# Token sums of squares by ones products over channel-major squares, with root and reciprocal on the spread values, in a two-layer transformer kernel on one core

## The chip, the cores and the metric

The kernel runs on 1 core of a Trainium2 chip. The metric is the device time of one execution in microseconds (us). The profiler names the engines PE (TensorE matmuls; PEld is its weight load), DVE (VectorE), ACT (ScalarE), POOL (GpSimd) and SP (the queue that issues the DMAs).

## The reference, cut to what matters

Two layers work on 1024 tokens of 256 channels. The second layer's MLP block contains an attention of its own, and that attention reads the layer-normalised activations after a second, root-mean-square normalisation:

```
h = _layernorm(x, axis=-1) * (1 + cb) + sb
x = x + gb * _L1_ffn_ref(h, ...)

def _L1_ffn_ref(hidden_states, ln1_w, ln2_w, Wq, ...):
    def _rmsnorm(x, w):
        v = jnp.mean(x * x, axis=-1, keepdims=True)
        return x * jax.lax.rsqrt(v + EPS) * w        # EPS = 1e-6
    x = _rmsnorm(hidden_states, ln1_w)
    attn = _attention(x, Wq, Wk, Wv, Wo)             # 16 heads, causal
    ...
    h = _rmsnorm(residual, ln2_w)
```

So one number per token is needed, 1 / sqrt(mean of its 256 squares + 1e-6), and it multiplies all channels of that token, before the q, k and v projections of this attention and again before the MLP.

## The kernel before, in words

Each engine has one program, written out in order, and the engines meet at semaphores (`S["name"]`, counted up by `then_inc`, awaited by `wait_ge`). There is no scheduler: the order in the code is the order on each engine. Only inside an attention is the order made by a small planner (`ORDER`), which the change leaves alone.

Activations live in two layouts. Token-major: 128 partitions are tokens, the channels lie along the row (`x`, `xn`). Channel-major: 128 partitions are channels, two chunks `dt` of 128 channels, 1024 tokens along the row, worked on in two halves of 512 tokens (`hT`, `h_hi`, `h_lo`, `rb`). The fp32 projections are made of three products of a high part and a low part (`mm3`, with `h_hi`, `h_lo`, `w_hi`, `w_lo`).

The place in question is `layer_norm(3)` and what follows it, ahead of `attention(1)`. DVE normalises `xn` (L1106), PE transposes it (L459), and ACT adds scale and shift and leaves channel-major `hT` in four pieces of 128 x 512 (L885; semaphore `ln_f`). Then the root-mean-square is taken:

1. PE transposes `hT` back to token-major (L819, 16 transposes, `u_t`).
2. ACT squares each of the 8 token tiles from PSUM, with an accumulated sum into a column of `ss` (L1050, `ss_ok`).
3. DVE makes mean + 1e-6 (L1457), ACT takes the root (L1053), DVE the reciprocal (L1459), all on 128 x 8 values.
4. DVE multiplies the identity by each tile's column (L1462, 8 times, `dg`), which gives diagonal matrices in `t1`; PE multiplies a matrix of ones by them (L824, `rb_m`), which spreads the value of each token over all 128 partitions; ACT copies that to `rb` (L1056, `rb_ok`).

Then `scaled_product` on DVE (L1210) makes `t2` = `hT` x `ln1_w` x `rb`, ACT rounds it to `h_hi` (L1060), and `scaled_low` on DVE (L1218) makes `h_lo`. For the first half PE waits until both its chunks have an `h_lo`:

```
for w in range(8):
    half, dt, is_k = w // 4, (w // 2) % 2, w % 2
    pe.wait_ge(S["ln_hl"], 12 + 2 * half + 2)
```

The eight products `w` (three kinds of row in each, L437 to L439) are q and k. Each is split into three bf16 parts (ACT L931 and L921, DVE L1193 and L1200), and SP writes the parts to a scratch in DRAM (L382) and loads them back in the layout of the attention (L391, 12 DMAs for a pair). PE meanwhile makes v (`token_major`) and then starts `attention(1)`, whose first matmuls (L743, L766) wait for those DMAs.

Of the kernel before, what the change touches and what calls it, by code (L numbers as in the profile page):

```python
# [7 lines left out]
ALU = mybir.AluOpType  # L8
ACT = mybir.ActivationFunctionType
# [7 lines left out]
P = 128  # L17
T = 1024
D = 256
H = 16  # L20
DH = D // H
NT = T // P
KC = D // P
HALF = 512
# [163 lines left out]
def build(nc, a, out):  # L188
# [13 lines left out]
    with ctx:  # L202
        def sb(name, shape, dt=F32):
            return ctx.enter_context(nc.sbuf_tensor(name, shape, dt))
# [4 lines left out]
        def overlay(*groups):  # L209
# [15 lines left out]
        hT = sb("hT", [P, KC, T])  # L225
# [31 lines left out]
        t1 = sb("t1", [P, 2, HALF])  # L257
        t2 = sb("t2", [P, 2, HALF])
# [18 lines left out]
        ve = sb("ve", [P, NT])  # L277
        sd = sb("sd", [P, NT])
        rs = sb("rs", [P, NT])
        ss = sb("ss", [P, NT])  # L280
        ident = sb("ident", [P, P])
        identb = sb("identb", [P, P], BF16)
        ones = sb("ones", [P, P])
        bd = sb("bd", [P, VW])
        minus1 = sb("minus1", [P, 1])
        tri = sb("tri", [P, P], BF16)
        rc = sb("rc", [P, 2, 2, 8])
        mx = sb("mx", [P, 2, 4, 4, 2])
# [13 lines left out]
        bank = [psum[:, i, :] for i in range(8)]  # L302
# [10 lines left out]
            att_t at_e wo_m ysem bt x_upd  # L313
            qt sp_h sp_r sp_m sp_l pw0 pw1 qr_ld0 qr_ld1 qr_ld2 qr_ld3 vp_e
            p1_s p1_mx m_max m_step m_t m_c m_ld0 m_ld1 s2 ex pv ob ot at_r
            u_t ss_ok ss_ve ss_sd ss_rs dg rb_m rb_ok a_f a_hi_s woa_m woa_ok ab
            z_m z_ok ha_m mm_f mm_h mm_ok bst h_f h_hi_s h_ok fs
            dq w_sc wf_t wf_h wf_l g_m u_m gl_s it_s it_h it_l fdn out_done""".split()
        names += [f"nat{i}" for i in range(FC[1])]
        S = {n: sem(n) for n in names}  # L320
# [112 lines left out]
        def _(pe):  # L433
# [148 lines left out]
            for j in range(4):  # L582
                m = modulation(wmod0, 0, 5, j)
# [11 lines left out]
            for t in range(NT):  # L595
# [8 lines left out]
                m = modulation(wmod0, 0, 3, 4 + t)  # L604
# [45 lines left out]
            for c in range(16):  # L650
                if c % 2 == 0 and c >= 4:
# [3 lines left out]
                    m = modulation(wmod1, 1, 7, (c - 4) // 2)  # L655
# [24 lines left out]
            for j in range(6, 12):  # L680
                m = modulation(wmod1, 1, 3, j)
# [20 lines left out]
            for w in range(8):  # L702
                half, dt, is_k = w // 4, (w // 2) % 2, w % 2
# [3 lines left out]
                for j in range(4):  # L707
                    c0 = is_k * D + dt * P
                    m = pe.transpose(bank[w % 4][:, j * P:(j + 1) * P], qk[:, 4 * half + j, c0:c0 + P], ident[:, :])
# [95 lines left out]
            for kc in range(KC):  # L805
                for o in range(KC):
                    m = pe.matmul(bank[1][:, kc * 96:(kc + 1) * 96], raw[:, 3, o, kc * P:(kc + 1) * P],
                                  a_rep[:, o, :], start=o == 0, stop=o == KC - 1)
# [3 lines left out]
            layer_norm(3)  # L812
            pe.wait_ge(S["wt_lo"], 10)
            pe.wait_ge(S["woa_ok"], 1)
            for v in range(4):
                pe.wait_ge(S["ln_f"], 12 + 2 * (v // 2) + 2)
                for j in range(2):
                    for dt in range(KC):
                        m = pe.transpose(bank[4 + v][:, j * D + dt * P:j * D + (dt + 1) * P],  # L819
                                         hT[:, dt, (2 * v + j) * P:(2 * v + j + 1) * P], ident[:, :])  # L820
                m.then_inc(S["u_t"], 1)
            for half in range(2):
                pe.wait_ge(S["dg"], 4 * half + 4)
                pe.matmul(bank[4 + half][:, :], ones[:, :], t1[:, half, :], start=True, stop=True  # L824
                          ).then_inc(S["rb_m"], 1)
            for w in range(8):
                half, dt, is_k = w // 4, (w // 2) % 2, w % 2
                pe.wait_ge(S["ln_hl"], 12 + 2 * half + 2)
# [2 lines left out]
                tok = slice(half * HALF, (half + 1) * HALF)  # L831
# [2 lines left out]
                    m = mm3(bank[w % 4][:, :], w_hi[:, kc, c0:c0 + P], w_lo[:, kc, c0:c0 + P],  # L834
                            h_hi[:, kc, tok], h_lo[:, kc, tok], kc == 0, kc == KC - 1)
                m.then_inc(S["qt"], 1)
            pe.wait_ge(S["rb_ok"], 2)
            for t in range(NT):
                if t >= 2:
                    pe.wait_ge(S["vp_e"], 8 + t - 1)  # L840
# [7 lines left out]
            for half in range(2):  # L848
                pe.wait_ge(S["h_ok"], 2 * half + 2)
                tok = slice(half * HALF, (half + 1) * HALF)  # L850
# [17 lines left out]
        def _(act):  # L868
# [174 lines left out]
            act.copy(woa[:, :, :], bank[1][:, 0:192].rearrange("p (c k) -> p c k", c=KC)).then_inc(S["woa_ok"], 1)  # L1043
            layer_norm_std(3)
            layer_norm_mod(3)
            for t in range(NT):
                act.wait_ge(S["u_t"], t // 2 + 1)
                if t >= 2:
                    act.wait_ge(S["ss_ok"], t - 1)
                act.activation(t2[:, t % 2, 0:D], bank[4 + t // 2][:, (t % 2) * D:(t % 2 + 1) * D], ACT.Square,  # L1050
                               accum_out=ss[:, t:t + 1]).then_inc(S["ss_ok"], 1)
            act.wait_ge(S["ss_ve"], 1)
            act.activation(sd[:, :], ve[:, :], ACT.Sqrt).then_inc(S["ss_sd"], 1)  # L1053
            for half in range(2):
                act.wait_ge(S["rb_m"], half + 1)
                act.copy(rb[:, half * HALF:(half + 1) * HALF], bank[4 + half][:, :]).then_inc(S["rb_ok"], 1)  # L1056
            for u in range(4):
                half, dt = divmod(u, 2)
                act.wait_ge(S["a_f"], u + 1)
# [18 lines left out]
        def _(ve_):  # L1078
            dve = ve_
# [373 lines left out]
            weight_lo(11, 9, 2 * D)  # L1453
            layer_norm(3)

            dve.wait_ge(S["ss_ok"], 8)
            dve.tensor_scalar(ve[:, :], ss[:, :], 1.0 / D, 1e-6, ALU.mult, ALU.add).then_inc(S["ss_ve"], 1)  # L1457
            dve.wait_ge(S["ss_sd"], 1)
            dve.reciprocal(rs[:, :], sd[:, :]).then_inc(S["ss_rs"], 1)  # L1459
            dve.wait_ge(S["ss_rs"], 1)  # L1460
            for t in range(NT):
                dve.tensor_scalar(t1[:, t // 4, (t % 4) * P:(t % 4 + 1) * P], ident[:, :], rs[:, t:t + 1], None, ALU.mult  # L1462
                                  ).then_inc(S["dg"], 1)

            for u in range(5):
                if u < 4:
# [28 lines left out]
        def _(pool):  # L1495
            pool.memset(ident[:, :], 0.0).then_inc(S["idz"], 1)
            pool.memset(bd[:, :], 1.0).then_inc(S["idz"], 1)
            pool.memset(minus1[:, :], -1.0)
            pool.memset(tri[:, :], 0.0).then_inc(S["idz"], 1)
            pool.wait_ge(S["idz"], 3)  # L1500
            pool.affine_select(out=ident[:, :], in_=ident[:, :], compare_op=ALU.not_equal, fill=1.0, base=0,
# [154 lines left out]
```

## Time and profile before

| | |
|---|---|
| median of 3 runs | 780.99 us (780.71 to 781.37) |
| the profiled execution: its own time | 780.97 us |
| its span, from first to last instruction | 779.4 us |
| PE busy | 676.7 us, 87% |
| DVE busy | 481.4 us, 62% |
| ACT busy | 334.0 us, 43% |
| POOL busy | 168.3 us, 22% |
| mean granted TensorE clock | 0.912 |

The span leaves 1.6 us of the execution's own time outside it. The granted clock is a share of 2.4 GHz, so 0.50 is 1.2 GHz. The shares of busy time are averages over stages that have different limits; the stage changed here lasts from about 509 to 529 us. An fp32 matmul of 128 x 512 stands as two records in the trace.

### The profile page before, as it was taken

Reading aid. Unit: us, or ns where it says so; the run is one execution under the profiler, and the core shown is the slowest. Engines: PE = TensorE matmul, PEld = TensorE weight load, DVE = VectorE, ACT = ScalarE, POOL = GpSimd, SP = SyncE. Lnnn points to the kernel's source line nnn. Section 1 sums busy time; section 2 is a strip of 40 time slices with the busy share of each in tenths; the row PEclk is TensorE's granted clock in tenths of the full one; section 3 lists DMA queues with packets and bytes.
Section 4 is the critical chain, followed back from the end, with each engine's and each line's share of the span. In section 5 each row is a group of like instructions: output and inputs, shape, how many; then the busy total and the mean of one; then the engine's idle time right before and its main releaser. Section 6 shows DMA issues by size and latency. Waiting matters only on the chain.

```text
span 779.4 us, 10833 instructions
## 1 busy us (share of the span) xinstructions
PE 676.7 (87%) x4017; PEld 447.2 (57%) x4017; DVE 481.4 (62%) x975; ACT 334.0 (43%) x539; POOL 168.3 (22%) x222
## 2 busy tenths in 40 slices
PE   5857996899999986747999998768799999999996
PEld 4645774677777775623544443447355444368885
DVE  5794367566666627966898850546688888232223
ACT  4213023433333342332555667456155566943332
POOL 1251122344455532910000000000000001002221
PEclk9995568999999997958999999969799999999999
DMA  9930001000000000066200000005730000050001
GB/s 215 245 114 1 0 2 54 1 1 0 1 1 1 0 1 1 6 191 210 84 2 1 1 2 1 0 1 162 229 98 2 1 1 1 3 162 1 1 1 54
DMA packets 47040, 36.18 MB, mean 46 GB/s; under 512 B 16206, under 2 KB 44892, under 8 KB 46988
## 3 DMA queue, kind: packets, MB, share of 16 engines
q1 hardware_dynamic: 46988, 35.49, 15.6%
q8 instruction: 32, 0.52, 0.3%
q14 instruction: 20, 0.16, 0.1%
HBM read 27.94 MB, written 7.34 MB: 45 GB/s over the span
## 4 chain that ended last, share of the span: by engine, by line
PE 42%; issue 21%; POOL 12%; DVE 11%; SPq 7%; DMA 3%; ACT 3%; POOLq 0%; DVEq 0%; ACTq 0%
PE psum L780 8%; POOL it_lo L1576 8%; PE psum L743 7%; PE psum L766 7%; SPq L391 4%; POOL wd L1559 3%; PE psum L627 2%; DVE qk L1172 2%; PE psum L639 2%; SPq L328 2%; PE psum L437 2%; PE psum L483 2%; PE psum L769 2%; DMA parts_scratch<-parts 2%; PE psum L439 2%
## 5 line engine op out<-in xcount | busy, mean ns | idle before, releaser
L957 ACT ACTIVATE pt<-psum 128x1024 f32<-128x1024 f32 (+1 forms) x192 | 147.9, 811 | 101.1 <-PE psum L769 72.6
L1256 DVE TENSOR_REDUCE mx<-psum 128x1 f32<-128x512 f32 (+3 forms) x216 | 132.6, 665 | 17.4 <-PE psum L743 8.9
L743 PE MATMUL psum<-kr,qr 96*128 96x512 bf16 (+3 forms) x384 | 111.1, 339 | 15.9 <-DMA kr<-parts_scratch 12.4
L766 PE MATMUL psum<-qr,kr 99*128 99x512 bf16 (+3 forms) x384 | 100.0, 333 | 9.2 <-DMA qr<-m3T 7.8
L1576 POOL TENSOR_TENSOR it_lo<-it,it_hi 128x512 fp32r<-128x512 f32 x48 | 67.1, 1398 | 165.5 <-ACT it_hi L995 164.3
L743 PEld LDWEIGHTS psum<-kr,qr 96*128 96x128 bf16 x384 | 37.0, 100 | 79.2 <-DVE mx L1256 30.5
L780 PE MATMUL psum<-pt,vp 128*32 128x512 f32 (+3 forms) x768 | 81.7, 498 | 0.0
L437 PE MATMUL psum<-h_hi,wf_hi 128*128 128x512 f32 x192 | 78.3, 408 | 3.1 <-issue 3.1
L439 PE MATMUL psum<-h_hi,wf_lo 128*128 128x512 f32 x192 | 75.5, 393 | 0.0
L438 PE MATMUL psum<-h_lo,wf_hi 128*128 128x512 f32 x192 | 75.3, 392 | 0.0
L1602 POOL TENSOR_SCALAR m<-m 128x16 bf16<-128x16 f32 x16 | 4.1, 254 | 307.0 <-DVE m L1256 153.5
L1326 DVE TENSOR_TENSOR it<-psum,gl 128x512 f32<-128x512 f32 x48 | 33.2, 691 | 60.0 <-PE psum L439 47.3
L1256 DVE TENSOR_REDUCE m<-psum 128x1 f32<-128x384 f32 (+3 forms) x88 | 50.9, 636 | 29.7 <-PE psum L746 29.1
L766 PEld LDWEIGHTS psum<-qr,kr 99*128 99x128 bf16 x384 | 35.9, 99 | 49.9 <-ACT pt L957 22.4
L995 ACT CAST it_hi<-it 128x512 fp32r<-128x512 f32 x48 | 29.8, 620 | 75.1 <-DVE it L1326 75.1
L1315 DVE TENSOR_TENSOR wf_lo<-psum,wf_hi 128x512 fp32r<-128x512 f32 (+1 forms) x48 | 24.5, 553 | 48.6 <-ACT wf_hi L981 48.6
L746 PE MATMUL psum<-tri,identb 128*128 128x128 bf16 x256 | 52.2, 230 | 0.0
L769 PE MATMUL psum<-identb,tri 128*128 128x128 bf16 x256 | 51.2, 223 | 0.0
L991 ACT ACTIVATE gl<-psum 128x512 f32<-128x512 f32 x48 | 28.7, 598 | 52.0 <-PE psum L439 33.9
L1533 POOL TENSOR_TENSOR t<-qk,rope_s 128x256 f32<-128x256 f32 x32 | 34.5, 1098 | 57.1 <-DVE qk L1353 23.5
L437 PEld LDWEIGHTS psum<-h_hi,wf_hi 128*128 128x128 f32 x192 | 36.5, 190 | 10.5 <-issue 3.6
L439 PEld LDWEIGHTS psum<-h_hi,wf_lo 128*128 128x128 f32 x192 | 36.4, 189 | 8.1
(194 smaller groups left out, 1203.9 us busy)
## 6 DMA issues: line engine op xcount, KB each, us to landing
parts_scratch<-parts SPq DMA_DIRECT2D x16, 384.0 KB, 3.3
qr<-parts_scratch SPq DMA_DIRECT2D x48, 128.0 KB, 2.6
kr<-parts_scratch SPq DMA_DIRECT2D x48, 128.0 KB, 2.6
wmod<-in_L_wmod SPq DMA_DIRECT2D x1, 1536.0 KB, 6.1
x<-in_L_attn_x SPq DMA_DIRECT2D x2, 512.0 KB, 4.0
wmod<-in_L_wmod SPq DMA_DIRECT2D x1, 1024.0 KB, 6.2
packed<-in_L_ffn_down_W_packed SPq DMA_DIRECT2D x1, 1024.0 KB, 10.1
nat<-in_L_ffn_W_in_base SPq DMA_DIRECT2D x8, 128.0 KB, 2.6
```

Of the source, the lines that this page charges most:

```text
L437: pe.matmul(dst, st_hi, mv_hi, start=first, stop=False)
L438: pe.matmul(dst, st_hi, mv_lo, start=False, stop=False)
L439: return pe.matmul(dst, st_lo, mv_hi, start=False, stop=last)
L743: m = pe.matmul(b, qr[0:PARTS_ROWS, c, h, (qt - 4 * c) * P:(qt - 4 * c + 1) * P], kr[0:PARTS_ROWS, ch, h, 0:w], start=True, stop=not diag)
L746: m = pe.matmul(b[:, w - P:w], identb[:, :], tri[:, :], start=False, stop=True)
L766: m = pe.matmul(bank[4 + 2 * at[0] + j][:, 0:w], kr[0:PARTS_ROWS + 3, kt // 4, h, (kt % 4) * P:(kt % 4 + 1) * P], qr[0:PARTS_ROWS + 3, c, ...
L769: m = pe.matmul(bank[4 + 2 * at[0] + j][:, 0:P], tri[:, :], identb[:, :], start=False, stop=True)
L780: m = pe.matmul(bank[3][32 * j:32 * j + 32, q0 - c * HALF:q0 - c * HALF + w], vp[:, kt, 4 * gp + j, :], pt[:, (n + j // 2) % 4, j % 2, 0:w ...
L957: act.activation(pt[:, n % 4, :, 0:w], psum[:, b:b + 2, 0:w], ACT.Exp, scale=0.25).then_inc(S["ex"], 1)
L1256: dve.tensor_reduce(dst, bank[at[0]][:, 0:k * w].rearrange("p (k w) -> p k w", k=k), AX, ALU.max).then_inc(S["p1_mx"], 1)
L1533: q = pool.tensor_tensor(v[0][:, :, i, :], v[1][:, :, 1 - i, :], s.unsqueeze(1).to_broadcast([P, 2 * H, DH // 2]), ALU.mult)
L1576: pool.tensor_tensor(it_lo[:, N % 2, :], it[:, N % 2, :], it_hi[:, N % 2, :].bitcast(F32), ALU.subtract).then_inc(S["it_l"], 1)
```

## The change

The sum of squares is taken without going back to token-major. ACT squares the four 128 x 512 pieces of `hT` directly (`Square`, from SBUF to SBUF) into `t1` (first half) and `t2` (second half). PE multiplies a matrix of ones by the squares, two matmuls a half that add up in one PSUM bank, so that each partition holds the sum over all 256 channels of each token. ACT takes the root of that, with scale 1/256 and a bias of 1e-6 from a new one-column tile `eps`, over 128 x 512 values, into `rb`. DVE takes the reciprocal of `rb` in place, 128 x 512 values a half. The 16 transposes, the 8 accumulated squares, the small row of operations on 128 x 8 values, the 8 diagonals and the two copies go.

```diff
+        eps = sb("eps", [P, 1])
...
-            for v in range(4):
-                pe.wait_ge(S["ln_f"], 12 + 2 * (v // 2) + 2)
-                for j in range(2):
-                    for dt in range(KC):
-                        m = pe.transpose(bank[4 + v][:, j * D + dt * P:j * D + (dt + 1) * P],
-                                         hT[:, dt, (2 * v + j) * P:(2 * v + j + 1) * P], ident[:, :])
-                m.then_inc(S["u_t"], 1)
-            for half in range(2):
-                pe.wait_ge(S["dg"], 4 * half + 4)
-                pe.matmul(bank[4 + half][:, :], ones[:, :], t1[:, half, :], start=True, stop=True
-                          ).then_inc(S["rb_m"], 1)
+            for half, sq in enumerate((t1, t2)):
+                pe.wait_ge(S["ss_ok"], 2 * half + 2)
+                for dt in range(KC):
+                    m = pe.matmul(bank[4 + half][:, :], ones[:, :], sq[:, dt, :], start=dt == 0, stop=dt == KC - 1)
+                m.then_inc(S["rb_m"], 1)
...
-            pe.wait_ge(S["rb_ok"], 2)
+            pe.wait_ge(S["ss_sd"], 2)
...
-            for t in range(NT):
-                act.wait_ge(S["u_t"], t // 2 + 1)
-                if t >= 2:
-                    act.wait_ge(S["ss_ok"], t - 1)
-                act.activation(t2[:, t % 2, 0:D], bank[4 + t // 2][:, (t % 2) * D:(t % 2 + 1) * D], ACT.Square,
-                               accum_out=ss[:, t:t + 1]).then_inc(S["ss_ok"], 1)
-            act.wait_ge(S["ss_ve"], 1)
-            act.activation(sd[:, :], ve[:, :], ACT.Sqrt).then_inc(S["ss_sd"], 1)
+            for u in range(4):
+                half, dt = divmod(u, 2)
+                act.wait_ge(S["ln_f"], 12 + u + 1)
+                act.activation((t1, t2)[half][:, dt, :], hT[:, dt, half * HALF:(half + 1) * HALF], ACT.Square
+                               ).then_inc(S["ss_ok"], 1)
             for half in range(2):
                 act.wait_ge(S["rb_m"], half + 1)
-                act.copy(rb[:, half * HALF:(half + 1) * HALF], bank[4 + half][:, :]).then_inc(S["rb_ok"], 1)
+                act.activation(rb[:, half * HALF:(half + 1) * HALF], bank[4 + half][:, :], ACT.Sqrt, scale=1.0 / D,
+                               bias=eps[:, :]).then_inc(S["ss_sd"], 1)
...
-            dve.wait_ge(S["ss_ok"], 8)
-            dve.tensor_scalar(ve[:, :], ss[:, :], 1.0 / D, 1e-6, ALU.mult, ALU.add).then_inc(S["ss_ve"], 1)
-            dve.wait_ge(S["ss_sd"], 1)
-            dve.reciprocal(rs[:, :], sd[:, :]).then_inc(S["ss_rs"], 1)
-            dve.wait_ge(S["ss_rs"], 1)
-            for t in range(NT):
-                dve.tensor_scalar(t1[:, t // 4, (t % 4) * P:(t % 4 + 1) * P], ident[:, :], rs[:, t:t + 1], None, ALU.mult
-                                  ).then_inc(S["dg"], 1)
+            for half in range(2):
+                dve.wait_ge(S["ss_sd"], half + 1)
+                tok = slice(half * HALF, (half + 1) * HALF)
+                dve.reciprocal(rb[:, tok], rb[:, tok]).then_inc(S["rb_ok"], 1)
+            dve.wait_ge(S["rb_m"], 2)
...
+            pool.memset(eps[:, :], 1e-6)
```

On DVE, right behind the last layer normalisation (`xn`), this stands before:

```order
L1106 TENSOR_SCALAR xn<-x,mv,rs 128x256 x8
L1457 TENSOR_SCALAR ve<-ss 128x8
L1459 RECIPROCAL rs<-sd 128x8
L1462 TENSOR_SCALAR t<-ident,rs 128x128 x8
L1210 SCALAR_TENSOR_TENSOR t<-hT,vec,rb 128x512 x2
L1218 TENSOR_TENSOR h_lo<-t,h_hi 128x512
```

And at the same place this stands now (the line numbers are those of the changed kernel, where `scaled_product` is L1202 and `scaled_low` L1210):

```order
L1098 TENSOR_SCALAR xn<-x,mv,rs 128x256 x8
L1451 RECIPROCAL rb<-rb 128x512 x2
L1202 SCALAR_TENSOR_TENSOR t<-hT,vec,rb 128x512 x2
L1210 TENSOR_TENSOR h_lo<-t,h_hi 128x512
```

Ten small operations have gone, and two reciprocals over 512 values a partition stand ahead of the first `scaled_product`, both of them, although that one needs only the first half of `rb`.

On ACT, between the four pieces of `hT` and the first rounding to `h_hi`, this stands before:

```order
L885 ACTIVATE hT<-psum,mod,onep 128x512 x4
L1050 ACTIVATE t,ss<-psum 128x256 x8
L1053 ACTIVATE sd<-ve 128x8
L1056 COPY rb<-psum 128x512 x2
L1060 CAST h_hi<-t 128x512 x4
```

And this now:

```order
L879 ACTIVATE hT<-psum,mod,onep 128x512 x4
L1043 ACTIVATE t<-hT 128x512 x4
L1047 ACTIVATE rb<-psum,eps 128x512 x2
L1052 CAST h_hi<-t 128x512 x4
```

Four squares over whole pieces take the place of eight with a sum, and the two copies have become two roots; no load of an activation table is added or removed there.

On PE, between the last transposes of `xn` and the first product of the q and k projection, the change is this:

```order
 L459 MATMUL psum<-ident,xn 128x128 x16
-L819 MATMUL psum<-ident,hT 128x128 x16
-L824 MATMUL psum<-t,ones 128x512 x2
+L818 MATMUL psum<-t,ones 128x512 x4
 L437 MATMUL psum<-h_hi,w_hi 128x512
 L438 MATMUL psum<-h_lo,w_hi 128x512
```

The transposes back to token-major have gone, and there are four ones products instead of two.

## Rows read from the trace of the kernel before

**Rows 1.** The page: the span, and busy time of PE.

```profile
span 779.4 us, 10833 instructions
...
PE 676.7 (87%) x4017; PEld 447.2 (57%) x4017; DVE 481.4 (62%) x975; ACT 334.0 (43%) x539; POOL 168.3 (22%) x222
```

**Rows 2.** The chain that ended last, 500 to 580: start us, length us, what.

```profile
509.87 0.41 ACT t L1050 x3
...
527.39 0.60 ACT parts L931
...
529.33 2.86 DMA parts_scratch<-parts
532.20 0.63 SPq L391
...
555.65 3.58 DMA qr<-m3T
559.27 0.61 PE psum L766
```

**Rows 3.** Timeline 505 to 543: start, length, instruction, [idle before <- releaser].

```profile
505.52 3.53 PE L459 MATMUL psum<-ident,xn 128*128 128x128 f32 x16 [4.97 <-DVE xn L1106]
...
509.77 0.37 ACT L1050 ACTIVATE t<-psum 128x256 f32<-128x256 f32 x1
...
514.43 2.64 PE L824 MATMUL psum<-t,ones 128*128 128x512 f32 x4 [3.42 <-DVE t L1462]
...
516.21 1.42 DVE L1210 SCALAR_TENSOR_TENSOR t<-hT,vec,rb 128x512 f32<-128x512 f32 x2 [1.05 <-ACT rb L1056]
517.11 0.59 ACT L1056 COPY rb<-psum 128x512 f32<-128x512 f32 x1 [0.93 <-PE psum L824]
517.59 1.14 ACT L1060 CAST h_hi<-t 128x512 fp32r<-128x512 f32 x2
518.24 0.69 DVE L1218 TENSOR_TENSOR h_lo<-t,h_hi 128x512 fp32r<-128x512 f32 x1 [0.62 <-ACT h_hi L1060]
...
520.45 0.79 PE L437 MATMUL psum<-h_hi,w_hi 128*128 128x512 f32 x1 [3.37 <-DVE h_lo L1218]
...
542.04 0.22 PE L743 MATMUL psum<-kr,qr 96*128 96x128 bf16 x1 [0.81 <-DMA kr<-parts_scratch]
```

**Rows 4.** The chain, 490 to 530: fp32 products of 128 x 512, 16 records.

```profile
489.77 6.87 PE psum L483 x16
```

**Rows 5.** Groups by shape on ACT: count | busy us, mean ns.

```profile
L896 ACT ACTIVATE hT<-psum,vec 128x512 f32<-128x512 f32 x4 | 2.4, 690 | 2.3 <-PE psum L474 2.3
```

**Rows 6.** Groups by shape on DVE: count | busy us, mean ns.

```profile
L1120 DVE TENSOR_TENSOR h_lo<-hT,h_hi 128x512 fp32r<-128x512 f32 x12 | 8.0, 685 | 0.0
...
L1384 DVE TENSOR_TENSOR xn<-psum,rc 128x256 f32<-128x256 f32 x8 | 3.3, 418 | 0.0
...
L1379 DVE RECIPROCAL rc<-rc 128x16 f32<-128x16 f32 x8 | 1.9, 244 | 0.0
...
L1459 DVE RECIPROCAL rs<-sd 128x8 f32<-128x8 f32 x1 | 0.2, 203 | 0.3 <-ACT sd L1053 0.3
```

**Rows 7.** Windows: length; busy PE, PEld, DVE, ACT, POOL; granted clock; DMA; GB/s.

```profile
511.00:514.40 3.40, 0.01 (x1) 0.00 (x0) 1.27 (x7) 1.99 (x11) 0.00 (x0) 1.00 0.03 5
514.40:517.10 2.70, 2.64 (x4) 0.67 (x4) 1.65 (x6) 0.59 (x1) 0.00 (x0) 0.73 0.00 0
517.10:520.40 3.30, 0.00 (x0) 0.00 (x0) 2.57 (x4) 2.20 (x4) 0.00 (x0) 0.50 0.00 0
520.40:525.70 5.30, 5.25 (x12) 4.13 (x13) 2.74 (x4) 1.24 (x3) 0.00 (x0) 0.50 0.00 0
525.70:530.00 4.30, 4.30 (x20) 3.52 (x19) 3.17 (x5) 3.31 (x6) 0.00 (x0) 0.98 0.20 67
```

**Rows 8.** Windows, same columns: two other restarts of PE at half clock.

```profile
343.80:348.30 4.50, 4.50 (x27) 2.65 (x28) 3.48 (x7) 0.00 (x0) 0.00 (x0) 0.50 0.50 166
...
559.40:563.40 4.00, 4.00 (x19) 2.32 (x18) 1.41 (x3) 1.52 (x2) 0.00 (x0) 0.50 0.68 206
```

More of the change, by code:

```diff
@@ L279, in build @@
         rs = sb("rs", [P, NT])
-        ss = sb("ss", [P, NT])
         ident = sb("ident", [P, P])
@@ L315, in build @@
             p1_s p1_mx m_max m_step m_t m_c m_ld0 m_ld1 s2 ex pv ob ot at_r
-            u_t ss_ok ss_ve ss_sd ss_rs dg rb_m rb_ok a_f a_hi_s woa_m woa_ok ab
+            ss_ok ss_sd rb_m rb_ok a_f a_hi_s woa_m woa_ok ab
             z_m z_ok ha_m mm_f mm_h mm_ok bst h_f h_hi_s h_ok fs
```

## The prediction

> **What bounds the kernel now.** I read the page first. PE is busy for 87% of the span of 779.4 us [rows 1], so a change off PE's path would cost or bring nothing. The second view is the chain that ended last. It runs through the changed stage without slack: from ACT's squares at 509.87 over the ones products and the first product of the q and k projection to ACT's split at 527.39, then to the DMA that writes the parts at 529.33, the row of reloads that SP issues from 532.20, and the DMA that ends PE's wait at 559.27 [rows 2]. So whoever asks what the edit is worth has to ask when PE can start the projection, which it does at 520.45 [rows 3], and how fast it then runs. PE itself has a wait of 0.81 us for the reloaded parts at 542.04 [rows 3], so it is the DMA row, not PE, that is last there; but both start from the same projection, and both move with it.
>
> The third view is the timeline of the stage, to see what fills the 10.7 us from 509.77 (ACT free of `hT`) to 520.45. The eight squares begin at 509.77, the ones products only at 514.43, the first `scaled_product` at 516.21; the second copy to `rb` stands on ACT at 517.11, ahead of the first rounding to `h_hi`, which begins at 517.59, and `h_lo` follows at 518.24 [rows 3]. The windows add the clock: PE is idle from 511.0 to 514.4 at full clock, the clock falls during the ones products (0.73 on average from 514.4 to 517.1), it is 0.50 over the next idle stretch, and stays 0.50 for the first 5.3 us of the projection [rows 7]. That is 1.2 GHz for 12 records; then 20 records go through in 4.3 us at 2.4 GHz, so a microsecond at half clock does half a microsecond's work.
>
> **The change, step by step.** I build the new timeline on the old clock time.
>
> 1. *Squares.* ACT is free at 509.77 as before. A square from SBUF to SBUF over 128 x 512 is not in the trace; the nearest row is the rounding to `h_hi`, same shape and same memories, two in 1.14 us [rows 3]. The first two end at 510.9, the other two 1.04 us later, at 511.95. Were it the price of an activation with a pointer, 0.69 us [rows 5], the first pair would end 0.1 us later. Nothing is cheaper in a way that matters: half the shape would not be enough to move the sum by more than 0.5.
> 2. *Ones products, first half.* Two fp32 matmuls are four records. Sixteen such records take 6.87 us at full clock [rows 4], 0.43 us apiece, so four take about 1.9 with the last one's tail: 511.0 to 512.9. PE has then been idle only since the transposes of `xn` end at 509.05 [rows 3]; in the old kernel it stayed at full clock through 3.4 us of idleness [rows 7], so full clock is the likelier reading. Their other half runs to 514.6.
> 3. *Root, first half.* From PSUM over 128 x 512 with a bias pointer: 0.69 us [rows 5]. 513.0 to 513.7.
> 4. *Reciprocal over 512 values a partition.* This is the dear and unknown term. The trace has reciprocals of 8 values (203 ns) and of 16 values (244 ns) [rows 6]. Eight more values cost 41 ns, 5.1 ns a value. Carried to 512, that is 0.203 + 504 x 0.0051 = 2.8 us each. The bounds: if a long reciprocal streamed like the two-operand product of the same shape it would be 0.69 us [rows 6]; if it took eight steps of the streaming interval a value it would be 4.4 us (below). I take the slope, since it comes from the operation itself, and with the small overlap of two neighbours 5.45 us for the pair: 513.7 to 519.15. What lies beside it: the squares, the products and the root of the second half (ready at about 515.4) are hidden under the first reciprocal, which ends near 516.5. Without that cover they would cost 1.7 us more.
> 5. *From `scaled_product` to PE.* Both reciprocals stand ahead of it on DVE, so it starts at 519.2 instead of 516.21. Behind it, one wait is gone: the rounding to `h_hi` no longer stands behind the second copy to `rb`. It starts when the first product ends (519.95, 0.62 us), and `h_lo` at 520.65, 1.45 us behind the `scaled_product` instead of 2.03. From the first `h_lo` to PE it was 2.21 us (518.24 to 520.45) [rows 3] and nothing in that piece changes. PE starts at 522.85: **2.4 us later**.
> 6. *The projection's clock.* PE will have been idle for some 8 us, so it starts at half clock, as it does now. How long that lasts is the second unknown. Here it was 5.3 us; at two other restarts in this trace 4.5 and about 4.1 [rows 7, 8]. The old case is the longest, so I expect 1.0 us less, which gives back **0.5 us**.
> 7. *The rest.* The 16 transposes ran on PE beside ACT's work and are worth nothing by themselves; the small operations are in the old chain and are already counted by rebuilding the timeline. One more memset on POOL at the start is one column wide and lies some 500 us ahead of its reader, so I cost it at nothing; the later reads of `rb`, before the MLP, are unchanged. Behind the projection everything hangs on the split and on SP's row of DMAs, all of which move by the same amount; only PE's 0.81 us could absorb something, and the chain does not pass through PE there.
>
> The sum is +2.4 - 0.5 = **+1.9 us**. The profiled execution took 780.97 us, 1.6 more than its span and the same as the median of 780.99 within 0.02, so I predict 782.9 us.
>
> A page speaks to the cost of the reciprocal. The row gives 41 ns for eight more values [rows 6]. The Trainium skill, "VectorE: DVE Perf Modes", walkthrough of the 8-slice pipeline, says that a reciprocal is an iterated hardware division with a repeat count of 8. Read as eight steps a value, eight values more would have cost 67 ns; the row shows 41, so the trace does not agree with that reading, but over only 16 values a fixed part may hide some of the slope. By the row the sum is +1.9; by the page read so it would be +5.2, the rival "eight steps".
>
> **The rivals.**
>
> - *Eight steps a value.* The streaming interval is (685 - 418) / 256 = 1.04 ns a value from the rows of 512 and of 256 [rows 6]; eight of them are 8.3 ns, 0.2 + 504 x 0.0083 = 4.4 us each, 8.7 for the pair, 3.3 more than in my sum: +5.2, 786.2 us. For it: a slope read off two short operations is weak evidence. Against it: it would have to show 67 ns where 41 stands. Chance 0.10.
> - *The clock rises as early as before.* The clock comes back at 525.7 whatever the start. Then the half-clock stretch is 2.9 us instead of 5.3, which gives back 1.2 us: +1.2, 782.2 us. For it: lengths of 4 to 5.3 us differ by more than a microsecond, so the start alone does not set the end. Against it: a rise after 2.9 us of work is in none of the rows that I show. Chance 0.17.
> - *The ones products fall into half clock.* PE does nothing from 509.05 to 511.0, and in the old kernel the clock fell during just these products. All four records of the first half at half clock cost 1.7 us more, about half of that is likely: +2.8, 783.8 us. Chance 0.09.
> - *The other side: a long reciprocal streams.* If the reciprocal is pipelined and its short-shape slope is start-up, it takes 0.69 us. The second one then waits for the second root (515.4), ends at 516.1, and PE starts at 519.8, 0.7 us earlier than now: 780.3 us, or 779.8 with a shorter half-clock stretch. It is not slower, and barely faster, since the second half's root is now in the way. The point that decides is a pair of 3.1 us, 2.6 ns a value, half of what the rows say. Chance 0.06.
>
> **How the numbers follow.** My own case, a reciprocal between 2.6 and 3.4 us and a delay between 1.2 and 3.4, has 0.58. What a measurement of this kernel can tell from no change is 0.2%, 1.6 us. My case lies above that except for its lower tail (0.09); with the eight steps and the half-clock products slower has 0.49 + 0.10 + 0.08 = 0.67. Same has the tail, the early clock and the streaming reciprocal, less a little: 0.29. Faster needs more than the streaming case gives, so 0.04 is left. The range reaches from 781.3 (the early clock, with the rest a little cheaper) to 786.2 (eight steps a value); below it lie the streaming case and the luck, above it half of the eight-step case.
>
> **What would show it.** In the new trace: two reciprocals of 128 x 512 on DVE of about 2.8 us each (0.7 or 4.4 would decide for a rival at once); squares of about 0.6 us ending near 512; four ones products of two records each at a granted clock near 1.00 between 511 and 514.6; the first projection matmul at 522.9 against 520.45, with DVE's reciprocals as the piece of the chain that replaces ACT's squares; and the length of the half-clock stretch behind it. The same delay must then stand at SP's first reload (532.20) and at PE's restart (559.27). I am wrong if the reciprocal's price per value at 512 is not that at 16, or if the clock behaves otherwise at the restart, there or at the one at 559.

## The result: 0.5% slower, twice the forecast cost

| | before | changed |
|---|---|---|
| median of 15 runs | 780.32 us (778.22 to 782.75) | 784.59 us (781.12 to 785.80) |
| span of the profiled execution | 779.4 us | 783.8 us |
| ratio of times, 95% interval | | 1.0052 (1.0038 to 1.0067) |

The change costs 4.1 us (0.0052 x 780.3) where I had +1.9. The time lies in the range, the direction was right, the size was not. I read the new trace as the old one. The page of the changed kernel, span and busy time, for [rows 1]:

```profile
span 783.8 us, 10784 instructions
...
PE 679.9 (87%) x4005; PEld 448.8 (57%) x4005; DVE 483.9 (62%) x967; ACT 333.3 (43%) x526; POOL 168.3 (21%) x223
```

DVE is busy 2.5 us more and ACT 0.7 us less; PE, which lost 16 transposes, is busy 3.2 us more. That total says nothing of the edit: between 100 and 200 us, far ahead of the changed stage, PE is busy 91.4 us against 87.3, at a granted clock of 0.85 against 0.88. The chain that ended last, over the changed stage, for [rows 2]:

```profile
510.31 1.04 ACT t L1043 x2
...
511.49 2.55 PE psum L818 x4
...
514.07 0.70 ACT rb L1047
...
514.79 3.41 DVE rb L1451 x2
518.20 3.07 issue
521.27 1.31 DVE t L1202 x2
...
524.81 0.80 PE psum L437
...
533.50 3.32 DMA parts_scratch<-parts
536.83 0.63 SPq L391
...
560.36 3.33 DMA qr<-m3T
563.73 0.61 PE psum L766
```

The squares of [rows 2] are gone; in their place stands a new piece from 514.79 to 521.27, the two reciprocals (the chain books the second half of it as "issue", but the timeline shows DVE busy throughout). The same stage in the timeline, for [rows 3]:

```profile
510.21 2.17 ACT L1043 ACTIVATE t<-hT 128x512 f32<-128x512 f32 x4
511.49 5.37 PE L818 MATMUL psum<-t,ones 128*128 128x512 f32 x8 [2.00 <-ACT t L1043]
514.07 0.69 ACT L1047 ACTIVATE rb<-psum,eps 128x512 f32<-128x512 f32 x1 [1.68 <-PE psum L818]
514.79 6.56 DVE L1451 RECIPROCAL rb<-rb 128x512 f32<-128x512 f32 x2 [7.74 <-ACT rb L1047]
516.90 0.69 ACT L1047 ACTIVATE rb<-psum,eps 128x512 f32<-128x512 f32 x1 [2.14 <-PE psum L818]
521.27 1.31 DVE L1202 SCALAR_TENSOR_TENSOR t<-hT,vec,rb 128x512 f32<-128x512 f32 x2
524.81 0.80 PE L437 MATMUL psum<-h_hi,w_hi 128*128 128x512 f32 x1 [7.95 <-DVE h_lo L1210]
```

And the clock, for [rows 7] (length; busy PE, PEld, DVE, ACT, POOL; granted clock; DMA; GB/s):

```profile
511.40:514.05 2.65, 2.56 (x5) 1.24 (x6) 0.00 (x0) 0.99 (x2) 0.00 (x0) 0.75 0.00 0
...
516.90:524.80 7.90, 0.00 (x0) 0.00 (x0) 7.73 (x7) 2.53 (x4) 0.00 (x0) 0.67 0.00 0
524.80:529.80 5.00, 4.99 (x12) 3.94 (x13) 2.74 (x4) 1.21 (x3) 0.00 (x0) 0.50 0.00 0
```

A stage is best compared on its own clock, since profiled executions differ by some tenths of a microsecond, and sometimes by several us, before it begins. I count from the first square on ACT. Before, PE starts the projection after 10.68 us (520.45 - 509.77) and SP issues the first reload after 22.43 (532.20 - 509.77). Changed, it is 14.60 (524.81 - 510.21) and 26.62 (536.83 - 510.21): 3.9 and 4.2 us later. The second figure agrees with the loss of 4.1 us, and at PE's restart after the DMA it is 4.0 (53.52 against 49.50, from 563.73 and 559.27).

### The profile page after: what moved, and what is told of

The parts are those of the page before. It is cut to its first block, busy times and chain, and to the rows that moved or that the text cites. A ratio compares the mean times of both kernels' runs of the same rounds, so it can differ in the third digit from the quotient of the medians.

```text
span 783.8 us, 10784 instructions
## 1 busy us (share of the span) xinstructions
PE 679.9 (87%) x4005; PEld 448.8 (57%) x4005; DVE 483.9 (62%) x967; ACT 333.3 (43%) x526; POOL 168.3 (21%) x223
## 4 chain that ended last, share of the span: by engine, by line
PE 43%; issue 22%; POOL 12%; DVE 10%; SPq 7%; DMA 3%; ACT 2%; POOLq 0%; DVEq 0%; ACTq 0%
PE psum L780 8%; POOL it_lo L1566 8%; PE psum L743 7%; PE psum L766 7%; SPq L391 4%; POOL wd L1549 3%; PE psum L627 2%; DVE qk L1164 2%; PE psum L639 2%; SPq L328 2%; PE psum L437 2%; PE psum L483 2%; PE psum L769 2%; DMA parts_scratch<-parts 2%; PE psum L438 2%
```

## The experiments

Each run's ratio is to the kernel before, measured with it; the changed kernel has 1.0052. The last two columns are the stage in the profiled execution, us from the first square to PE's first projection record and to SP's first reload. They come from one execution each, and two things in them change from execution to execution. One is the half-clock stretch at the start of the projection: from 3.2 us (half_first, hybrid, before_half) over 4.4 (no_recip, ladder), about 5 (changed) and 5.3 (before, transposes_back) to 6.1 (half_first_2), and where PE is last a microsecond of it costs about half a microsecond (below, warm_start loses 5.3 us of it and gains 2.5). The other is the DMA ahead of the first reload: 3.32 us in the changed kernel's trace, 3.01 in ladder and 2.84 to 2.86 in all others, so the reload of the changed kernel stands some 0.5 us too late in this table.

| run | ratio (95% interval) | PE starts | first reload |
|---|---|---|---|
| before | 1 | 10.68 | 22.43 |
| changed | 1.0052 (1.0038 to 1.0067) | 14.60 | 26.62 |
| no_recip | 1.0002 (0.9983 to 1.0021) | 11.38 | 22.78 |
| half_first | 1.0042 (1.0026 to 1.0058) | 12.92 | 25.23 |
| half_first_2 | 1.0010 (0.9995 to 1.0025) | 10.31 | 22.67 |
| half_first_warm | 1.0008 (0.9981 to 1.0034) | 10.25 | 22.62 |
| transposes_back | 1.0039 (1.0026 to 1.0052) | 13.96 | 25.68 |
| warm_start | 0.9996 (0.9982 to 1.0009) | 13.95 | 23.20 |
| hybrid | 1.0038 (1.0020 to 1.0056) | 15.86 | 26.66 |
| hybrid_warm | 0.9987 (0.9968 to 1.0005) | 13.08 | 22.35 |
| before_warm | 0.9947 (0.9924 to 0.9970) | 10.08 | 19.33 |
| before_half | 0.9992 (0.9972 to 1.0013) | 9.50 | 20.21 |
| before_half_warm | 0.9945 (0.9922 to 0.9968) | 9.51 | 18.76 |

### ladder: what a reciprocal costs by its length

```diff
             update(3)
+            dve.memset(t1[:, :, :], 1.5).then_inc(S["lad"], 1)
+            dve.wait_ge(S["lad"], 1)
+            at = 0
+            for n in (8, 16, 32, 64, 128, 256):
+                dve.reciprocal(t2[:, 0, at:at + n], t1[:, 0, at:at + n]).then_inc(S["lad"], 1)
+                at += n
+            dve.reciprocal(t2[:, 1, :], t1[:, 1, :]).then_inc(S["lad"], 1)
+            dve.tensor_scalar(h_lo[:, 0, 0:HALF], t1[:, 1, :], 1.0, None, ALU.mult).then_inc(S["lad"], 1)
```

> The changed kernel with a measurement added at its very end, after all else on VectorE: reciprocals of 8, 16, 32, 64, 128, 256 and 512 values a partition, and one multiplication by 1.0 over 512. Theory A (every value costs the same and the short ones hide a part of it in their start): the steps between 32, 64, 128, 256 and 512 lie on one line of about 6.3 ns a value that ends at the 3.3 us seen in the changed kernel, and only the step from 8 to 16 is smaller. Theory B (long ones are dearer a value, as if something else were slow at 512 values in place): the step from 8 to 16, 5 ns a value, holds up to 128 or 256 and the last step is steeper. The whole kernel is longer by the sum of these, about 7 us, which is not of interest.

Groups by shape on DVE in this run (count | busy us, mean ns):

```profile
L1487 DVE RECIPROCAL t<-t 128x512 f32<-128x512 f32 x1 | 3.3, 3296 | 0.0
...
L1371 DVE RECIPROCAL rc<-rc 128x16 f32<-128x16 f32 x8 | 2.0, 245 | 0.0
L1485 DVE RECIPROCAL t<-t 128x256 f32<-128x256 f32 x1 | 1.7, 1695 | 0.0
L1485 DVE RECIPROCAL t<-t 128x128 f32<-128x128 f32 x1 | 0.9, 897 | 0.0
...
L1485 DVE RECIPROCAL t<-t 128x64 f32<-128x64 f32 x1 | 0.5, 496 | 0.0
L1485 DVE RECIPROCAL t<-t 128x32 f32<-128x32 f32 x1 | 0.3, 296 | 0.0
L1485 DVE RECIPROCAL t<-t 128x8 f32<-128x8 f32 x1 | 0.2, 204 | 0.0
L1485 DVE RECIPROCAL t<-t 128x16 f32<-128x16 f32 x1 | 0.2, 201 | 0.0
```

From 32 to 512 all steps lie on one line: (496 - 296) / 32 = 6.25 ns a value, (897 - 496) / 64 = 6.27, (1695 - 897) / 128 = 6.23, (3296 - 1695) / 256 = 6.25. Theory A holds. The step below is what misled me: 8 and 16 values cost the same here (204 and 201 ns), and in the same trace the 16 values of `rc` still take 245. So the 41 ns between 8 and 16 in [rows 6] were a difference between two places in the program, not a price per value; what makes `rc` dearer is not shown. The whole kernel took 789.01 us in its one run, with 7 us of ladder in it.

### no_recip: the reciprocals left out

```diff
-                dve.reciprocal(rb[:, tok], rb[:, tok]).then_inc(S["rb_ok"], 1)
+                dve.tensor_scalar(rb[:, tok], rb[:, tok], 1.0, None, ALU.mult).then_inc(S["rb_ok"], 1)
```

> The changed kernel with each of the two reciprocals over 512 values replaced by a multiplication by 1.0 of the same tile in place (the reciprocal is left out, so the tokens are scaled by the root and not by its inverse). Theory 1 (the reciprocals are what the change costs): scaled_product starts when the second root is done, near 517.7 instead of 521.3, so 3.3 to 3.6 us come back and the time is 781 us, about 0.7 above the kernel before, the rest being the ones products at half clock. Theory 2 (the clock of TensorE is what it costs, at the products and at the restart): less than 1.5 us come back, and the time stays above 783.

Two rows of its timeline, the multiplications in the reciprocals' place and the first scaled product:

```profile
514.61 0.43 DVE L1451 TENSOR_SCALAR rb<-rb 128x512 f32<-128x512 f32 x1 [2.27 <-ACT rb L1047]
514.95 1.41 DVE L1202 SCALAR_TENSOR_TENSOR t<-hT,vec,rb 128x512 f32<-128x512 f32 x2
```

The ratio falls from 1.0052 to 1.0002, 3.9 us, and the reload comes 3.8 us earlier in the stage (26.62 to 22.78). Theory 1 is met, theory 2 (less than 1.5 us back) is out. Note what is last now: DVE waits 2.27 us for the second root. So 3.2 us is what PE's start gains, less than the 6.56 us of the pair, because the second half's products and root come out from under the first reciprocal. And even with a pass of 0.43 us in the place of each reciprocal the new form, in this order, is level with the old one; a cheap pass together with the order of half_first_2 was not run.

### half_first, half_first_2: the second reciprocal off the first half's path

```diff
+            dve.wait_ge(S["rb_m"], 2)
             for half in range(2):
                 dve.wait_ge(S["ss_sd"], half + 1)
                 tok = slice(half * HALF, (half + 1) * HALF)
                 dve.reciprocal(rb[:, tok], rb[:, tok]).then_inc(S["rb_ok"], 1)
-            dve.wait_ge(S["rb_m"], 2)
+                for u in (2 * half, 2 * half + 1):
+                    scaled_product(u, 5, "a_f", "ln_hl", 12)
+                for u in (2 * half, 2 * half + 1):
+                    scaled_low(u, "a_hi_s", "ln_hl")
...
-            for u in range(5):
-                if u < 4:
-                    scaled_product(u, 5, "a_f", "ln_hl", 12)
-                if u >= 1:
-                    scaled_low(u - 1, "a_hi_s", "ln_hl")
```

> The changed kernel with VectorE's order changed: reciprocal, the two scaled products and the two low parts of the first half, then the same for the second half. Theory 1: PE starts the projection 3.3 us earlier, but VectorE then comes later to the split (second reciprocal and four more operations end at about 527.3, and five split operations follow), so the DMA of the parts is 2.5 to 3 us earlier: 782 us. Theory 2: the start moves by 3.3 us but the half-clock stretch grows by as much, so less than 1.5 us come back.

That diff is half_first: the wait stands ahead of the first reciprocal, which therefore starts with the end of the second ones product and not of the first root. PE starts 1.7 us earlier (12.92 against 14.60), not the 3.3 that both theories had, and 1.4 us arrive at the reload, 0.5 of it the DMA of the table. The ratio of 1.0042 misses the 782 us of theory 1 (1.002), and theory 2 is not tested, since its start did not happen. In half_first_2 the wait is the first thing behind the reciprocal instead:

> The run before this one on VectorE's order had a fault of mine: its wait for both ones products stood ahead of the first reciprocal and held it back by 2.3 us. Here the wait stands behind the first reciprocal. Theory 1 (the place of the reciprocals on the path is what counts): against the changed kernel PE starts the projection 3.3 us earlier and the first DMA reload is 2.5 us earlier or more, so about 0.3% comes back: ratio to the kernel before 1.002. Theory 2 (what VectorE does later, the second reciprocal in front of the split, costs as much as the start gains): ratio 1.004 again.

DVE's timeline in half_first_2 (start, length, instruction):

```profile
511.92 3.35 DVE L1451 RECIPROCAL rb<-rb 128x512 f32<-128x512 f32 x1 [7.07 <-ACT rb L1047]
515.39 1.41 DVE L1202 SCALAR_TENSOR_TENSOR t<-hT,vec,rb 128x512 f32<-128x512 f32 x2
516.83 1.35 DVE L1210 TENSOR_TENSOR h_lo<-t,h_hi 128x512 fp32r<-128x512 f32 x2
518.10 3.34 DVE L1451 RECIPROCAL rb<-rb 128x512 f32<-128x512 f32 x1
521.53 1.41 DVE L1202 SCALAR_TENSOR_TENSOR t<-hT,vec,rb 128x512 f32<-128x512 f32 x2
522.97 1.35 DVE L1210 TENSOR_TENSOR h_lo<-t,h_hi 128x512 fp32r<-128x512 f32 x2
524.24 1.28 DVE L1185 TENSOR_TENSOR xn<-psum,parts 128x512 f32<-128x512 f32 x2
```

The second reciprocal now runs beside PE's projection. PE starts after 10.31 us and the reload after 22.67, 4.0 us sooner than in the changed kernel; the ratio is 1.0010, somewhat better than I expected. So the loss was not the reciprocals' length alone, but that both stood ahead of a product that needs only one. In this execution the ones products also kept full clock, which is 0.6 of the 4.3 us at PE's start, though the code ahead of them is that of the changed kernel:

```profile
509.21 3.67 PE L818 MATMUL psum<-t,ones 128*128 128x512 f32 x8 [2.00 <-ACT t L1043]
```

No row of DVE is preceded by idle time from 515.39 on: the engine is full up to the split. The chain that ends in the first reload runs over DVE's second products and the split (from 521.53) and over no projection record.

### transposes_back, warm_start: what PE's idleness costs

```diff
             pe.wait_ge(S["woa_ok"], 1)
+            for v in range(4):
+                pe.wait_ge(S["ln_f"], 12 + 2 * (v // 2) + 2)
+                for j in range(2):
+                    for dt in range(KC):
+                        m = pe.transpose(bank[4 + v][:, j * D + dt * P:j * D + (dt + 1) * P],
+                                         hT[:, dt, (2 * v + j) * P:(2 * v + j + 1) * P], ident[:, :])
             for half, sq in enumerate((t1, t2)):
...
                 m.then_inc(S["rb_m"], 1)
+            for _ in range(8):
+                pe.matmul(bank[7][:, :], ones[:, :], t1[:, 0, :], start=True, stop=True)
```

The upper piece alone is transposes_back, both are warm_start. Nothing reads what they write.

> The changed kernel with the 16 transposes of hT put back on PE between the transposes of xn and the ones products, with no reader: PE is busy from 509.1 to 511.1 again, as before. Theory 1: the granted clock during the ones products was lost by the idle stretch that the removed transposes left; with them back all eight records run at 2.4 GHz, the first half takes 1.9 us instead of 2.55, and 0.6 us come back: 783.9 us. Theory 2: the clock falls there anyway, and the time is that of the changed kernel, 784.6 us, or 0.1 us longer.

> The changed kernel with the 16 transposes put back and with 8 ones products without a reader on PE behind the two that count, so that PE is busy for about 7 us of the time in which VectorE makes its reciprocals. Theory 1: the projection then starts at 2.4 GHz, its first 12 records take 2.8 us instead of 5.1, the first reload comes 2.3 us earlier beside the 0.6 us of the transposes, and the ratio to the kernel before is 1.001 to 1.002. Theory 2 (the clock at the restart is not on the path, since the DMAs wait for VectorE's and ScalarE's split): the reload moves by less than 1 us and the ratio is that of transposes_back, 1.004.

The ones products of transposes_back:

```profile
508.05 3.70 PE L824 MATMUL psum<-t,ones 128*128 128x512 f32 x8
...
510.79 3.35 DVE L1457 RECIPROCAL rb<-rb 128x512 f32<-128x512 f32 x1 [6.96 <-ACT rb L1053]
```

Eight records in 3.70 us instead of 5.37, and PE starts the projection 0.64 us earlier. The ratio goes from 1.0052 to 1.0039, in the right direction, though the two intervals overlap. That the removed transposes had kept the clock up fits theory 1, but is not shown. Without them the eight records took 5.37 us in four traces (changed, ladder, no_recip, half_first) and 3.67 in one, half_first_2, behind the same 2.00 us of idleness; with them it was 3.62 to 3.70 in all three (transposes_back, warm_start, half_first_warm). So they may make full clock likelier; they are not needed for it.

Windows of warm_start (same columns as before), the products, the fillers, the gap, the projection:

```profile
507.80:511.50 3.70, 3.70 (x11) 1.72 (x10) 0.90 (x1) 1.74 (x4) 0.00 (x0) 1.00 0.02 4
511.50:518.40 6.90, 6.90 (x17) 2.75 (x15) 6.90 (x4) 1.30 (x2) 0.00 (x0) 1.00 0.00 0
518.40:520.60 2.20, 0.03 (x1) 0.00 (x0) 2.04 (x3) 1.21 (x2) 0.00 (x0) 1.00 0.00 0
520.60:525.00 4.40, 4.38 (x19) 3.65 (x20) 3.45 (x6) 2.34 (x5) 0.00 (x0) 1.00 0.00 0
```

PE starts at the same place in the stage (13.95 against 13.96), but at 2.4 GHz, and the reload comes 2.5 us earlier. The ratio is 0.9996, better than the 1.001 to 1.002 of theory 1: matmuls that nothing reads bring the changed kernel level with the old one. Theory 2, that the clock is not on the path, is out for this order of work. It does not follow that the clock was the loss, since the old kernel gains as much from such matmuls (before_warm, below).

### half_first_warm: the same fillers where DVE is late

This is half_first_2 with the 16 transposes and four of the fillers.

> half_first_2 with the transposes put back and four ones products without a reader behind the two that count. In half_first_2 VectorE was busy without a gap from the first scaled product to the split, the second reciprocal in it, so VectorE and not PE is late there. Theory 1: a faster projection is worth nothing, only the 0.6 us of the first product and root can come back: ratio 1.000, against 1.001. Theory 2: the clock is worth its 2.3 us here as well: ratio 0.998.

The ratio is 1.0008 against 1.0010, and the reload 22.62 against 22.67. The timeline shows why, with one row of PE and four of DVE:

```profile
519.29 3.35 DVE L1459 RECIPROCAL rb<-rb 128x512 f32<-128x512 f32 x1
519.43 0.50 PE L437 MATMUL psum<-h_hi,w_hi 128*128 128x512 f32 x1 [1.92 <-DVE h_lo L1218]
...
522.73 1.42 DVE L1210 SCALAR_TENSOR_TENSOR t<-hT,vec,rb 128x512 f32<-128x512 f32 x2
524.17 1.36 DVE L1218 TENSOR_TENSOR h_lo<-t,h_hi 128x512 fp32r<-128x512 f32 x2
525.44 1.28 DVE L1193 TENSOR_TENSOR xn<-psum,parts 128x512 f32<-128x512 f32 x2
```

The projection's records are short now, but DVE gets to the split only when the second reciprocal and its four products are done. In warm_start 5.3 us at half clock were taken away and the reload came 2.5 us earlier; here it is 6.1 us and the reload comes 0.05 us earlier. That also answers why half_first_2 ends level with the old kernel and not ahead of it, though PE starts 0.4 us earlier: the second reciprocal is off the first half's path, but not off DVE.

### hybrid, hybrid_warm: the new squares, the old small values

```diff
+                for j in range(4):
+                    for dt in range(KC):
+                        m = pe.matmul(bank[4 + half][:, j:j + 1], sq[:, dt, j * P:(j + 1) * P], ones[:, 0:1],
+                                      start=dt == 0, stop=dt == KC - 1)
+                m.then_inc(S["u_t"], 1)
```

> A version of my own: the squares of the changed kernel (four, channel-major), but the sums by products with the squares as the weights and one column of ones, which gives the sums token-major as 128 x 8 values; then the old mean, root, reciprocal and diagonals over few values, each half by itself, and the old ones product and copy. Theory 1: no reciprocal over 512 values, and the first half's row begins at 511 instead of 512.7, so PE starts the projection 1.4 us earlier than in the kernel before: ratio 0.998. Theory 2: the 16 small products with a weight load each and the semaphores between the engines eat that: ratio 1.000.

> The version before this one with six ones products without a reader that keep PE busy: two before the sums, one between the sums and the spread, three between the spread and the projection. Theory 1: the projection starts at 2.4 GHz, 2.3 us more than hybrid: ratio 0.995. Theory 2: the clock still falls, since PE is idle between the fillers, or the fillers delay what counts: ratio as hybrid, 0.998, or worse.

Both theories for hybrid failed: 1.0038, PE's start 5.2 us later than before instead of 1.4 earlier. The row that decides:

```profile
512.38 6.17 PE L818 MATMUL psum<-ones,t 128*128 128x1 f32 x32 [2.11 <-ACT t L1048]
```

A product with one column is 0.19 us a record all the same, and 32 of them took longer than the eight records of the changed kernel. Each brings a new 128 x 128 fp32 weight, and PEld is busy for 6.08 of the 6.17 us, so the weights are what fills them. The granted clock was 0.57 there; the spread (519.79) then starts 4.0 us later in the stage than in the old kernel and takes 3.78 us at 0.52 instead of 2.64. With fillers (hybrid_warm) the ratio is 0.9987, short of theory 1's 0.995: the 32 records take 3.73 us at full clock, 0.12 apiece, and the projection starts at 2.4 GHz. But the fillers did not hold the clock throughout. It was 0.50 from 518.5 to 521.5, among the spread products, behind the 32 one-column records and 1.10 us of filler, with no idle stretch of PE over 0.3 us since 513.6.

### before_warm, before_half, before_half_warm: the old form, improved

before_warm puts three ones products without a reader ahead of the old spread and three behind it; before_half makes mean, root, reciprocal and diagonals of a half as soon as its four tiles are squared:

```diff
+            for _ in range(3):
+                pe.matmul(bank[3][:, :], ones[:, :], hT[:, 0, 0:HALF], start=True, stop=True)
             for half in range(2):
                 pe.wait_ge(S["dg"], 4 * half + 4)
                 pe.matmul(bank[4 + half][:, :], ones[:, :], t1[:, half, :], start=True, stop=True
                           ).then_inc(S["rb_m"], 1)
+            for _ in range(3):
+                pe.matmul(bank[3][:, :], ones[:, :], t1[:, 0, :], start=True, stop=True)
```

That is before_warm; and this, on DVE, before_half:

```diff
+            for half in range(2):
+                cols = slice(4 * half, 4 * half + 4)
+                dve.wait_ge(S["ss_ok"], 4 * half + 4)
+                dve.tensor_scalar(ve[:, cols], ss[:, cols], 1.0 / D, 1e-6, ALU.mult, ALU.add).then_inc(S["ss_ve"], 1)
+                dve.wait_ge(S["ss_sd"], half + 1)
+                dve.reciprocal(rs[:, cols], sd[:, cols]).then_inc(S["ss_rs"], 1)
```

> The kernel before, with three ones products without a reader on PE while ScalarE squares, and three more behind the spread. It changes nothing but PE's activity. Theory 1 (the half-clock start of the projection is on the path of both kernels): the projection runs at 2.4 GHz from its first record, 12 records take 2.8 us instead of 5.1, the spread products keep full clock (0.7 us), and the ratio to the kernel before is 0.996 to 0.997. Theory 2 (the fillers delay the products that count, or the clock falls in the gap all the same): 1.000.

> The kernel before, with mean, root, reciprocal and diagonals of each half as soon as its four tiles are squared; no operation over 512 values. Theory 1: the first half's spread begins 1.0 us earlier, PE starts the projection 1.0 us earlier: ratio 0.9987. Theory 2: the extra small operations and the second half's row behind them eat it: 1.000.

> before_half with two ones products without a reader on PE ahead of the spread and three behind it. Theory 1: both gains add up, 1.0 and some 2.5 us: ratio 0.9955. Theory 2: only the clock or only the halves count: 0.997 to 0.999.

before_warm has 0.9947 (0.9924 to 0.9970), 4.1 us less than the kernel before and a little better than the 0.996 to 0.997 of theory 1, which its interval includes. Its stage is 3.1 us shorter (22.43 to 19.33): 0.6 at PE's start, and the rest about half of the 5.3 us at half clock that are gone. Its granted clock:

```profile
509.00:512.00 3.00, 2.16 (x5) 0.61 (x5) 2.03 (x10) 0.68 (x5) 0.00 (x0) 1.00 0.00 0
512.00:515.00 3.00, 3.00 (x8) 1.41 (x8) 2.08 (x3) 2.36 (x4) 0.00 (x0) 1.00 0.00 0
515.00:518.00 3.00, 2.14 (x8) 1.24 (x7) 2.73 (x5) 1.25 (x2) 0.00 (x0) 1.00 0.00 0
518.00:521.00 3.00, 3.00 (x15) 2.46 (x14) 2.18 (x4) 1.74 (x4) 0.00 (x0) 1.00 0.00 0
```

before_half moved PE's start by 1.2 us, near the 1.0 expected, but its ratio of 0.9992 cannot be told from 1 nor from the 0.9987 expected. Its profiled execution shows a reload 2.2 us earlier, more than the start explains: the half-clock stretch was 3.2 us instead of 5.3 in that execution. before_half_warm, at 0.9945, cannot be told from before_warm; the halves add nothing that these runs resolve.

Set side by side, the two forms with a warm projection differ as much as the two without: warm_start 0.9996 against before_warm 0.9947, 0.5% with intervals that lie apart, and 23.20 against 19.33 at the reload, 3.9 us. The clock is a gain that both forms can have; the reciprocals are what the new form loses.

## Why the prediction was right in sign and short in size

- **Step 1, squares**: right. 2.17 us for four against my 2.18.
- **Step 2, first ones products**: the wrong choice between two readings. The clock fell among them (0.75 over the first half's), and four records took 2.55 us instead of 1.9: 0.65 us more. This was the rival "the ones products fall into half clock", which I gave 0.09, arguing that the old kernel kept full clock through a longer idle stretch. That idle stretch had 16 transposes just ahead of it, which the edit removes, and step 7 puts them at nothing; transposes_back fits that as the cause, but half_first_2 kept full clock without them, so the cause stays open.
- **Step 3, root**: right, 0.69 us. The Trainium skill, "ScalarE: Activation LUTs", section "What ACT_TABLE_LOAD costs", gives 280 + 0.833 N ns for an activation with a bias pointer, an estimate of 707 ns here; the trace has 687, so it agrees within 3%.
- **Step 4, reciprocal**: the term that was mis-sized most. I wrote "I take the slope, since it comes from the operation itself": 5.1 ns a value, 5.45 us for the pair. It is 6.25 ns and 6.56 us, 1.1 us more. The slope came from two operations that cost the same when they stand side by side (ladder), and the prediction's own sign of being wrong, a price per value at 512 that is not that at 16, has come true. That the second half's products and root hide under the first reciprocal was right. The rival in which a long reciprocal streams had the right time, level with the old kernel (no_recip, 1.0002), but not the way: it had PE start after 10.0 us (519.8), and no_recip has 11.38, with the eight ones-product records at 5.37 us instead of 3.6. The Trainium skill, "VectorE: DVE Perf Modes", walkthrough of the 8-slice pipeline, states a repeat count of 8 and no time; my reading of it, eight steps of 1.04 ns, is too dear, the ladder gives six (6.25 / 1.04).
- **Step 5, scaled product to PE**: right. Before 4.24 us (516.21 to 520.45), forecast 3.65, measured 3.54 (521.27 to 524.81).
- **Step 6, the clock at the restart**: the mechanism right, the size not. I expected 4.3 us at half clock and it was 5.0, so 0.15 us came back instead of 0.5. The forecast took the mean of a few restarts for the next one; the traces of this case spread from 3.2 to 6.1 us.
- **Step 7**: the rest moved with it, as said. The first DMA of the parts took 3.32 us instead of 2.86, which adds 0.46. No other trace has more than 3.01, so I put it down to this execution and not to the edit.

The sum closes: 2.4 + 1.1 + 0.65 = 4.15 for PE's start, less 0.1 in step 5 and 0.1 in rounding, measured 3.92; to the reload, less 0.2 for the shorter half-clock stretch, plus 0.46 for the DMA, 4.2. The delay of 3.9 us at PE lies outside the 1.2 to 3.4 of my own case. That the time fell in the range was in part luck: the upper end stood for a reciprocal of eight steps, which did not happen, and covered two smaller errors with the same sign.

What is shown: that the reciprocals are the loss (no_recip, and the two warm forms side by side), that their price is linear (ladder), that their place matters as much as their length (half_first_2), and that half-clock matmuls are on the path here (warm_start) and off it once DVE is late (half_first_warm). What stays open: how long the half-clock stretch will be in a given execution. It was 3.2 to 6.1 us in nine traces at nearly the same place, and I have no run that sets it. Open too is what decides the clock of the ones products.

## What to carry to other kernels

Take a root or a reciprocal on the few values and spread afterwards, if the few values can be had cheaply (hybrid's sums cost more than they saved): spreading first turned 8 values a partition into 1024, and at 6.25 ns each on DVE that is 6.6 us for an edit that removed ten operations. Do not extrapolate a price per value from operations of 8 and 16 values; put both ends of such a guess in the sum, or find a row above 32. And when PE work that looks useless goes, ask what clock the next matmul will be granted: six ones products without a reader were worth 0.5% here (before_warm), as much as the edit cost, but only where PE and not another engine is last.

## What the runs showed of the hardware

- A reciprocal on DVE costs 6.25 ns a value from 32 to 512 values a partition (296 to 3296 ns), and no less than about 0.2 us at 8 and 16.
- A multiplication by a number over the same 512 values in place took 0.43 us, an eighth of it.
- An fp32 product of one column with a new 128 x 128 weight each time took 0.19 us a record over 32 records at a granted clock of 0.57 (hybrid), and 0.12 at 1.00 (hybrid_warm).
- With matmuls that nothing reads around them, idle stretches of PE of 2.2 us (warm_start) and 0.6 to 0.9 us (before_warm, before_half_warm) passed at a granted clock of 1.00, and PE's start was not later for them. In hybrid_warm, with such matmuls too, the clock fell to 0.50 for 3 us behind 32 one-column records.
- The same program ahead of the same place was granted full clock in one trace and less in others: eight ones-product records in 3.67 us (half_first_2) and in 5.37 (no_recip, half_first).
